# TensorE's signals raised by a drain of its sequencer, in a graph network of four layers

## The chip, the cores and the metric

One NeuronCore of one Trainium2 chip runs the whole program. The metric is the device time of one execution in microseconds (us); lower is better. The core has five engines that run side by side, each with its own queue of instructions: PE (TensorE, matrix products), DVE (VectorE), ACT (ScalarE), POOL (GpSimd) and SP (SyncE, which here only issues DMAs). They wait for each other by semaphores.

## The reference

`x` holds 6,250 nodes of 128 values; there are 106,250 edges with `src`, `dst` (sorted by `dst`) and one of 40 types. Each of four layers computes `x = LayerNorm(x + layer(x))`:

- layer 0, relations: `S = segment_sum(x[src], dst * 40 + type)`, then `sum over r of S[:, r] @ W[r]` plus `cnt @ rFeatures`, times `deg ** -0.5`, then `relu(h + h @ loop)`;
- layer 1, attention with 4 heads of 64: a softmax over the edges of each target, with `segment_max` as its maximum, weighted `segment_sum`, relu, a product by `fc_w`;
- layer 2, attention with 4 heads of 32, with one global maximum, a skip, elu;
- layer 3, six rounds of routing on 8 capsules of 16 values: `p = softmax(sum(z * u[dst]))` per edge with `z = xk[src]`, `u = normalize(segment_sum(z * p, dst) + xk)`.

## The kernel before

The edges are laid into 880 chunks of 128 slots (`NCH`), taken four at a time: a *quad* (`CQ = 4`, `NQ = 220`). A gather or scatter by index is an indirect DMA that POOL issues, one per chunk. A sum over targets is a product on PE of a 0/1 matrix (*hots*, made from `dst`) by the rows of the chunk. Most buffers exist four times (`RING`), indexed by `s = q % 4`. `sweep()` (L53) writes out the order on each engine: for each quad it calls the stage functions, each at an offset of so many quads. A function waits on its semaphores, issues, and lets its last instruction raise one. The program's order on each engine is this written order.

The five stages that the diff touches (letters are this document's):

- **A, the products of layer 0** (L451 to L510). For each of 50 node tiles, ACT copies the tile to `xs` (L480), PE transposes it (L491, raises `s_xtp`), ACT copies it to `xt` (L484), and PE makes ten products of 128 x 512 (L497, each raises `s_y`) into four PSUM banks in turn; product n waits for the addition of n - 4 (`s_yc`). DVE adds the relation features (L509) into `y_out`, and SP stores two additions at a time (L463) to `y_tab`. On POOL, beside this and independent of it, 831 scatters (L472) write the edge records.
- **B, the sums of layer 0** (L749 to L827). POOL gathers the edges' rows of `y_tab` (L562), DVE makes hots (L599), PE's `total` multiplies four chunks (L827, raises `s_sum` once a quad), DVE adds each chunk's sum to its target tile (L813).
- **C, the maximum of layer 1** (`source_maximum`, L1012 to L1124). POOL gathers (L1035), ACT packs (L1088), PE's `turn` transposes (L1108, `s_turn`), ACT copies a line (L1096), PE's `spread` makes for each chunk four products (L1118) and one (L1121, `s_spread` per chunk), DVE reduces each chunk (L1067). PE's order is turn of q + 1, spread of q.
- **D, layer 2's sweep** (`attend_once`, L1413 to L1564). PE's order for quad q: `expand` of q + 1 (L1532, `s_exp`), `turn` of q + 1 (L1542, `s_turn`), `lanes` of q (L1548, `s_row`), `spread_top` (L1552, `s_bc`), `total` (L1561, `s_sum`). Between them DVE needs expand for `sent` (L1440), the scores and their maximum over lanes (L1454), PE turns that to a row, DVE takes the running maximum (L1458, L1461), PE spreads it, ACT makes the exponential, DVE the messages (L1468), then comes the total. POOL gathers ahead (L562), as buffers come free.
- **E, round one of layer 3** (`first_round`, L1796 to L1970). PE's order: `total` of q - 1 (L1963, `s_sum`), `turn` of q + 1 (L1953, `s_turn`), `expand` of q + 2 (L1942, `s_exp`). POOL gathers `z` (L1827), DVE makes products, sums and messages (L1845, L1865) and adds (L1881), ACT widens, exponentiates and scales hots (L1904, L1912, L1922).

In all five POOL issues indirect DMAs. The stages without them (the sweep over kept rows in layer 1, rounds two to six of layer 3 with L2227 and L2239, the projections) are not touched. A `drain` of an engine is an instruction of its sequencer that stands in the program's order behind the others; before the change the touched blocks have one on each engine at their end only.

Of the kernel before, what the change touches and what calls it, by code (L numbers as in the profile page):

```python
# [14 lines left out]
P = 128  # L15
# [68 lines left out]
def gnn_resnorm_kernel(nc, x_in, src_in, dst_in, type_in, rfeat, relw, loopw,  # L84
# [3 lines left out]
    with ctx:  # L88
# [59 lines left out]
        with Phase() as ph:  # L148
# [302 lines left out]
            with nc.Block() as block:  # L451
                @block.sync
                def _(sp):
                    sp.dma_start(w0[:], relw.rearrange("r d f -> d r f")).then_inc(s_w, 16)
                    sp.dma_start(rf_b[:], rfeat.rearrange("r d -> (r d)").unsqueeze(0).broadcast_to([P, R * D]))\
                      .then_inc(s_w, 16)
                    sp.wait_ge(s_w, 32)


                    for d in range(NTP * GRP // 2):  # L460
                        t, c = d // (GRP // 2), d % (GRP // 2)
                        sp.wait_ge(s_yc, 2 * d + 2)
                        sp.dma_start(y_view[t:t + 1, :, c * 1024:(c + 1) * 1024].rearrange("t p w -> (t p) w"),  # L463
                                     y_out[:, d % 2].rearrange("p a w -> p (a w)")).then_inc(s_yo[d % 2], 16)
                    for s in range(2):
                        sp.wait_ge(s_yo[s], 16 * (NTP * GRP // 4))

                @block.gpsimd
                def _(pool):

                    for j in range(EJ):
                        nc.gpsimd.indirect_dma_start(  # L472
                            out=rec_tab, out_offset=bass.IndirectOffsetOnAxis(ap=row_i[:, j:j + 1], axis=0),
                            in_=pay[:, j, :], in_offset=None).then_inc(s_sc, 16)
                    pool.wait_ge(s_sc, 16 * EJ)

                @block.scalar
                def _(act):
                    for t in range(NTP):
                        nc.scalar.activation(xs[:], x_sb[:, t, :], ACT.Copy).then_inc(s_xs, 1)  # L480
                        act.wait_ge(s_xtp, t + 1)
                        if t > 0:
                            act.wait_ge(s_y, t * GRP)
                        nc.scalar.activation(xt[:], ps[:, 7, 0:P], ACT.Copy).then_inc(s_xt, 1)  # L484

                @block.tensor
                def _(pe):
                    pe.wait_ge(s_w, 32)
                    for t in range(NTP):
                        pe.wait_ge(s_xs, t + 1)  # L490
                        nc.tensor.transpose(ps[:, 7, 0:P], xs[:], ident[:]).then_inc(s_xtp, 1)  # L491
                        pe.wait_ge(s_xt, t + 1)
                        for g in range(GRP):
                            n = t * GRP + g
                            if n > 3:
                                pe.wait_ge(s_yc, n - 3)
                            nc.tensor.matmul(ps[:, n % 4, :], xt[:], w0[:, 4 * g:4 * g + 4, :],  # L497
                                             start=True, stop=True).then_inc(s_y, 1)

                @block.vector  # L500
                def _(dve):
                    v = nc.vector
                    dve.wait_ge(s_w, 32)
                    for n in range(NTP * GRP):
                        g, d = n % GRP, n // 2
                        dve.wait_ge(s_y, n + 1)
                        if n % 2 == 0 and d >= 2:
                            dve.wait_ge(s_yo[d % 2], 16 * (d // 2))
                        v.tensor_tensor(y_out[:, d % 2, n % 2, :], ps[:, n % 4, :],  # L509
                                        rf_b[:, g * 512:(g + 1) * 512], ALU.add).then_inc(s_yc, 1)  # L510
# [220 lines left out]
        with Phase() as ph:  # L731
# [17 lines left out]
            with nc.Block() as block:  # L749
# [69 lines left out]
                @block.tensor  # L819
                def _(pe):  # L820
                    def total(q, s):
                        pe.wait_ge(s_hot, q + 1)
                        pe.wait_ge(s_gath[s], gathered(q, s))
                        if not isinstance(q, int) or q >= 2:
                            pe.wait_ge(s_acc, (q - 1) * CQ)
                        for c in range(CQ):
                            last = nc.tensor.matmul(ps[:, (s % 2) * CQ + c, 0:W], hots[:, s, c, :], ring[:, s, c, :],  # L827
                                                    start=True, stop=True)
                        last.then_inc(s_sum, 1)
                    sweep(pe, [(0, total)], straight=True)  # L830


# [146 lines left out]
        def source_maximum(name, f, t_tab, keep_tab, most):  # L979
# [5 lines left out]
            with Phase() as ph:  # L985
# [26 lines left out]
                with nc.Block() as block:  # L1012
# [86 lines left out]
                    @block.tensor  # L1099
                    def _(pe):  # L1100
                        pe.wait_ge(s_ini, 2)

                        def turn(q, s):
                            pe.wait_ge(s_pack, q + 1)
                            if not isinstance(q, int) or q >= 2:
                                pe.wait_ge(s_line, q - 1)
                            pe.sem_inc(s_tick, 1)
                            nc.tensor.transpose(turned(s), parts[:, s, :], ident_b[:])\  # L1108
                              .then_inc(s_turn, 1)

                        def spread(q, s):
                            pe.wait_ge(s_line, q + 1)
                            pe.wait_ge(s_oth, q + 1)
                            for c in range(CQ):
                                if not isinstance(q, int) or q >= 1:
                                    pe.wait_ge(s_red, (q - 1) * CQ + (c + 1))
                                for h in range(HEADS):
                                    nc.tensor.matmul(ps[:, c, h * P:(h + 1) * P], pick[:, c * HEADS + h, :],  # L1118
                                                     lines[:, s, :], start=h == 0, stop=False)

                                nc.tensor.matmul(ps[:, c, :], others[:, s, c, :],  # L1121
                                                 far[:].rearrange("p h e -> p (h e)"), start=False, stop=True)\
                                  .then_inc(s_spread, 1)
                        sweep(pe, [(1, turn), (0, spread)], straight=True)  # L1124

        def target_rows(name, ph, a_src, a_dst, most, exp_n, own):
# [228 lines left out]
        def attend_once(name, f, t_tab, a_dst, last_neg, top_neg):  # L1355
# [6 lines left out]
            with Phase() as ph:  # L1362
# [50 lines left out]
                with nc.Block() as block:  # L1413
# [109 lines left out]
                    def _(pe):  # L1523
# [3 lines left out]
                        def expand(q, s):  # L1527
# [3 lines left out]
                            for c in range(CQ):  # L1531
# [1 line left out]
                                    ps[:, 6 + s % 2, c * HW:(c + 1) * HW], ohts[:, s, c * P:(c + 1) * P],  # L1533
                                    exp_n[:, bass.ds(tiles[s, c], 1), :, :].rearrange("p t k w -> p (t k w)"),
                                    start=True, stop=True)
                            last.then_inc(s_exp, 1)

                        def turn(q, s):
                            if not isinstance(q, int) or q >= 2:
                                pe.wait_ge(s_hot, q - 1)  # L1540
                            for c in range(CQ):
                                last = nc.tensor.transpose(turned(s)[:, c * P:(c + 1) * P],  # L1542
                                                           ohts[:, s, c * P:(c + 1) * P], ident_b[:])
                            last.then_inc(s_turn, 1)

                        def lanes(q, s):
                            pe.wait_ge(s_lt, q + 1)
                            nc.tensor.transpose(lane_row(s), lane_top[:, s, :], ident[:]).then_inc(s_row, 1)  # L1548

                        def spread_top(q, s):  # L1550
                            pe.wait_ge(s_rt, q + 1)
                            nc.tensor.matmul(spread(s), one_row[:], run_top[0:1, s:s + 1], start=True, stop=True)\  # L1552
                              .then_inc(s_bc, 1)

                        def total(q, s):
                            pe.wait_ge(s_m, q + 1)
# [3 lines left out]
                            for c in range(CQ):  # L1560
                                last = nc.tensor.matmul(sums(s, c), hots[:, s, c, :], msg[:, s, c, :],  # L1561
                                                        start=True, stop=True)
                            last.then_inc(s_sum, 1)
                        sweep(pe, [(1, expand), (1, turn), (0, lanes), (0, spread_top), (0, total)], tiles, straight=True)  # L1564


# [144 lines left out]
        with Phase() as l3:  # L1711
# [47 lines left out]
            def first_round(name):  # L1759


                with Phase() as ph:
# [33 lines left out]
                    with nc.Block() as block:  # L1796
# [136 lines left out]
                        def _(pe):  # L1933
                            def body(r):
                                tiles = Tiles(PE_ENGINE, 2)

                                def expand(q, s):
# [3 lines left out]
                                    for c in range(CQ):  # L1941
# [1 line left out]
                                            ps[:, s, c * D:(c + 1) * D], wide[:, s, c * P:(c + 1) * P],  # L1943
                                            unit[:, bass.ds(tiles[s, c], 1), :].rearrange("p t w -> p (t w)"),
                                            start=True, stop=True)
                                    last.then_inc(s_exp, 1)

                                def turn(q, s):
                                    pe.wait_ge(s_ohl[s], r * per + loaded(q, s))
# [2 lines left out]
                                    for c in range(CQ):  # L1952
                                        last = nc.tensor.transpose(turned(s)[:, c * P:(c + 1) * P],  # L1953
                                                                   ohts[:, s, c * P:(c + 1) * P], ident_b[:])
                                    last.then_inc(s_turn, 1)

                                def total(q, s):
                                    pe.wait_ge(s_msg, r * NQ + (q + 1))
# [3 lines left out]
                                    for c in range(CQ):  # L1962
                                        last = nc.tensor.matmul(ps[:, 4 + s % 2, c * D:(c + 1) * D], hots[:, s, c, :],  # L1963
                                                                msg[:, s, c * D:(c + 1) * D], start=True, stop=True)
                                    last.then_inc(s_sum, 1)
                                sweep(pe, [(-1, total), (1, turn), (2, expand)], tiles, straight=True)
                            body(0)

# [340 lines left out]
```

## Time and profile before

| | |
|---|---|
| median of 3 runs | 11,336.08 us (11,329.6 to 11,339.88) |
| the profiled execution | 11,339.56 us, of which the span 11,337.8 us |
| busy share of the span | PE 60%, DVE 57%, POOL 57%, PE's weight loads 45%, ACT 22% |
| mean granted clock of PE | 0.703 of full speed |
| L562 POOL gathers of B | 881.7 us busy (1,002 ns each), 726.4 us idle before them |
| L472 POOL scatters of A | 842.3 us busy (1,014 ns each) |
| L497 PE products of A | 607.2 us busy, 821.8 us idle before them |
| L509 DVE additions of A | 330.9 us busy, 1,124.8 us idle before them, 794.4 of it "remote" |

"Idle before" is the time an engine sat idle just ahead of those instructions, with what ended most of it; idle time of an engine that is not the bottleneck costs nothing. "issue" means that the engine waited for nothing that the profile shows, "remote" that a semaphore was waited for whose sender was not found. Two matmul records belong to one fp32 product.

### The profile page before, as it was taken

Reading aid. Unit: us, or ns where it says so; the run is one execution under the profiler, and the core shown is the slowest. Engines: PE = TensorE matmul, PEld = TensorE weight load, DVE = VectorE, ACT = ScalarE, POOL = GpSimd, SP = SyncE. Lnnn points to the kernel's source line nnn. Section 1 sums busy time; section 2 is a strip of 40 time slices with the busy share of each in tenths; the row PEclk is TensorE's granted clock in tenths of the full one; section 3 lists DMA queues with packets and bytes.
Section 4 is the critical chain, followed back from the end, with each engine's and each line's share of the span. In section 5 each row is a group of like instructions: output and inputs, shape, how many; then the busy total and the mean of one; then the engine's idle time right before and its main releaser. Section 6 shows DMA issues by size and latency. Waiting matters only on the chain. (4 is left out here: it accounts for less than half of the span.)

```text
span 11337.8 us, 161595 instructions
## 1 busy us (share of the span) xinstructions
PE 6767.9 (60%) x41381; PEld 5071.3 (45%) x41382; DVE 6482.6 (57%) x18631; ACT 2515.4 (22%) x6766; POOL 6430.9 (57%) x5741
## 2 busy tenths in 40 slices
PE   4422256333337777688745555345444698898986
PEld 3200022333323333344434444244444698898986
DVE  7411135555555555677754444534444688888888
ACT  0000000000010000022211111133333455555554
POOL 0477732777726666444235555255555587787876
PEclk9755577555565555599865555577776899999998
DMA  0111135555546666655322222233333566666664
GB/s 22 58 47 46 46 145 184 117 115 117 113 80 172 176 175 176 167 181 182 115 53 62 61 61 62 40 97 97 95 97 96 145 210 186 186 210 187 209 186 149
DMA packets 1109223, 1395.56 MB, mean 123 GB/s; under 512 B 277691, under 2 KB 974351, under 8 KB 1108111
## 3 DMA queue, kind: packets, MB, share of 16 engines
q1 hardware_dynamic: 955182, 1090.46, 31.1%
q0 software_dynamic: 153312, 296.65, 12.9%
q8 instruction: 304, 4.98, 0.2%
q14 instruction: 425, 3.47, 0.1%
HBM read 1002.58 MB, written 383.96 MB: 122 GB/s over the span
## 5 line engine op out<-in xcount | busy, mean ns | idle before, releaser
L562 POOL DMA_INDIRECT ring_e<-t_tab,src_row x880 | 832.4, 946 | 825.6 <-DVE msg_e L1468 424.1
L1827 POOL DMA_INDIRECT z_r<-x_tab,src_row x880 | 839.4, 954 | 805.6 <-DVE msg_r L1865 405.1
L562 POOL DMA_INDIRECT ring<-y_tab,y_row x880 | 881.7, 1002 | 726.4 <-DVE ring L783 356.5
L472 POOL DMA_INDIRECT rec_tab<-pay,row_i x831 | 842.3, 1014 | 694.5 <-POOLq L202 402.1
L2227 PE MATMUL ps<-u,wide_r 128*128 x9280 | 1141.4, 277 | 126.2 <-issue 88.7
L2239 PE MATMUL ps<-msg_r,hots_r 128*128 128x128 f32 x9280 | 1150.8, 277 | 105.4 <-POOL msg_r L2060 104.7
L2060 POOL TENSOR_TENSOR msg_r<-zo_r,share_r 128x1024 f32<-128x1024 f32 x580 | 1122.8, 1936 | 87.5 <-DVE share_r L2119 13.7
L2227 PEld LDWEIGHTS ps<-u,wide_r 128*128 128x128 f32 x9280 | 1093.0, 194 | 128.2 <-issue 128.2
L2239 PEld LDWEIGHTS ps<-msg_r,hots_r 128*128 128x128 f32 x9280 | 1083.2, 192 | 138.4 <-POOL msg_r L2060 137.7
L1035 POOL DMA_INDIRECT ring_m<-t_tab,src_row x880 | 850.5, 966 | 516.7 <-ACT slot_parts_m L1088 262.9
L497 PE MATMUL ps<-w,xt 128*128 128x512 f32 x1000 | 607.2, 747 | 821.8 <-issue 503.7
L2068 POOL TENSOR_TENSOR prod_r<-prod_r 128x512 f32<-128x512 f32 x580 | 735.1, 1267 | 437.4 <-DVE prod_r L2091 425.1
L509 DVE TENSOR_TENSOR y_out<-ps,rf_b 128x512 f32<-128x512 f32 x500 | 330.9, 689 | 1124.8 <-remote 794.4
L827 PE MATMUL ps<-ring,hots 128*128 128x129 f32 x1760 | 458.6, 442 | 835.4 <-issue 561.1
L1067 DVE TENSOR_REDUCE high_m<-ps 128x4 f32<-128x512 f32 x880 | 588.9, 685 | 623.4 <-PE ps L1121 348.3
L827 PEld LDWEIGHTS ps<-ring,hots 128*128 128x128 f32 x1760 | 394.1, 329 | 900.1 <-issue 679.0
L497 PEld LDWEIGHTS ps<-w,xt 128*128 128x128 f32 x1000 | 207.4, 228 | 1202.8 <-issue 672.4
L1118 PE MATMUL ps<-lines_m,pick_m 48*128 48x128 bf16 x3520 | 530.5, 304 | 350.2 <-DVE high_m L1067 273.5
L2091 DVE TENSOR_TENSOR prod_r<-ps,zo_r 128x1024 f32<-128x1024 f32 x580 | 707.9, 1221 | 33.3 <-PE ps L2227 30.8
L2130 DVE TENSOR_TENSOR u_sum<-ps,u_sum 128x128 f32 x2320 | 667.4, 288 | 89.5 <-PE ps L2239 40.2
L1561 PE MATMUL ps<-msg_e,hots_e 128*128 128x132 f32 x1760 | 468.2, 447 | 333.9 <-DVE msg_e L1468 333.9
L1963 PE MATMUL ps<-msg_r,hots_r 128*128 128x128 f32 x1760 | 341.4, 355 | 509.9 <-DVE msg_r L1865 395.2
(320 smaller groups left out, 13430.4 us busy)
## 6 DMA issues: line engine op xcount, KB each, us to landing
zo_r<-zo_tab SPq DMA_DIRECT2D x2320, 192.0 KB
y_tab<-y_out SPq DMA_DIRECT2D x250, 512.0 KB
k_tab<-ring_m SPq DMA_DIRECT2D x220, 520.0 KB
ring_e<-k_tab SPq DMA_DIRECT2D x220, 520.0 KB
ohts_e<-oht_tab SPq DMA_DIRECT2D x440, 128.0 KB
zo_tab<-z_r SPq DMA_DIRECT2D x220, 256.0 KB
dl_b<-dl_tab SPq DMA_DIRECT2D x220, 128.0 KB
oht_tab<-ohts SPq DMA_DIRECT2D x220, 128.0 KB
```

The costliest lines, as they stand in the source:

```text
L472: nc.gpsimd.indirect_dma_start(out=rec_tab, out_offset=bass.IndirectOffsetOnAxis(ap=row_i[:, j:j + 1], axis=0), in_=pay[:, j, :], in_offse ...
L497: nc.tensor.matmul(ps[:, n % 4, :], xt[:], w0[:, 4 * g:4 * g + 4, :], start=True, stop=True).then_inc(s_y, 1)
L562: nc.gpsimd.indirect_dma_start(out=ring[:, s, c, 0:width], out_offset=None, in_=table, in_offset=bass.IndirectOffsetOnAxis(ap=rows[:, q * ...
L827: last = nc.tensor.matmul(ps[:, (s % 2) * CQ + c, 0:W], hots[:, s, c, :], ring[:, s, c, :], start=True, stop=True)
L1035: nc.gpsimd.indirect_dma_start(out=ring[:, s, c, :], out_offset=None, in_=t_tab, in_offset=bass.IndirectOffsetOnAxis(ap=src_row[:, q * CQ ...
L1827: nc.gpsimd.indirect_dma_start(out=z[:, s, c * D:(c + 1) * D], out_offset=None, in_=x3_tab, in_offset=bass.IndirectOffsetOnAxis(ap=src_row ...
L2060: nc.gpsimd.tensor_tensor(msg[:, g % WR].rearrange("p c (k d) -> p c k d", d=CD), z_of(g).rearrange("p c (k d) -> p c k d", d=CD), share[: ...
L2068: nc.gpsimd.tensor_tensor(prod[:, :, 0:CD // 2], prod[:, :, 0:CD // 2], prod[:, :, CD // 2:CD], ALU.add).then_inc(s_half, 1)
L2091: v.tensor_tensor(prod[:].rearrange("p (c k) d -> p c (k d)", k=CAPS), up, z_of(g), ALU.mult).then_inc(s_prod, 1)
L2130: v.tensor_tensor(t, ps[:, 4 + g % 2, a * D:(a + 1) * D], t, ALU.add)\
L2227: last = nc.tensor.matmul(ps[:, 2 * (g % 2) + c // 4, c % 4 * D:(c % 4 + 1) * D], wide[:, g % WR, c, :], u[:, bass.ds(tiles[g % NO % 4 * O ...
L2239: last = nc.tensor.matmul(ps[:, 4 + g % 2, c // 2 * D:(c // 2 + 1) * D], hots[:, g % WR, c, :], msg[:, g % WR, c, :], start=c % 2 == 0, st ...
```

## The change

In the five stages every `then_inc` on a matmul or transpose is removed, and a `nc.tensor.drain()` behind it raises the same semaphore by the same amount. Order, waits, operands and all other engines are as they were. The drains number 50 + 500 in A, 220 in B, 220 + 880 in C, 5 x 220 in D and 3 x 220 in E.

```diff
@@ stage A: the products of layer 0 @@
-                        nc.tensor.transpose(ps[:, 7, 0:P], xs[:], ident[:]).then_inc(s_xtp, 1)
+                        nc.tensor.transpose(ps[:, 7, 0:P], xs[:], ident[:])
+                        nc.tensor.drain().then_inc(s_xtp, 1)
...
                             nc.tensor.matmul(ps[:, n % 4, :], xt[:], w0[:, 4 * g:4 * g + 4, :],
-                                             start=True, stop=True).then_inc(s_y, 1)
+                                             start=True, stop=True)
+                            nc.tensor.drain().then_inc(s_y, 1)
@@ stage B: total @@
                             last = nc.tensor.matmul(ps[:, (s % 2) * CQ + c, 0:W], hots[:, s, c, :], ring[:, s, c, :],
                                                     start=True, stop=True)
-                        last.then_inc(s_sum, 1)
+                        nc.tensor.drain().then_inc(s_sum, 1)
@@ stage C: turn, and spread (once a chunk) @@
-                            nc.tensor.transpose(turned(s), parts[:, s, :], ident_b[:])\
-                              .then_inc(s_turn, 1)
+                            nc.tensor.transpose(turned(s), parts[:, s, :], ident_b[:])
+                            nc.tensor.drain().then_inc(s_turn, 1)
...
                                 nc.tensor.matmul(ps[:, c, :], others[:, s, c, :],
-                                                 far[:].rearrange("p h e -> p (h e)"), start=False, stop=True)\
-                                  .then_inc(s_spread, 1)
+                                                 far[:].rearrange("p h e -> p (h e)"), start=False, stop=True)
+                                nc.tensor.drain().then_inc(s_spread, 1)
@@ stage D: expand, turn, lanes, spread_top, total @@
-                            last.then_inc(s_exp, 1)
+                            nc.tensor.drain().then_inc(s_exp, 1)
...
-                            last.then_inc(s_turn, 1)
+                            nc.tensor.drain().then_inc(s_turn, 1)
...
-                            nc.tensor.transpose(lane_row(s), lane_top[:, s, :], ident[:]).then_inc(s_row, 1)
+                            nc.tensor.transpose(lane_row(s), lane_top[:, s, :], ident[:])
+                            nc.tensor.drain().then_inc(s_row, 1)
...
-                            nc.tensor.matmul(spread(s), one_row[:], run_top[0:1, s:s + 1], start=True, stop=True)\
-                              .then_inc(s_bc, 1)
+                            nc.tensor.matmul(spread(s), one_row[:], run_top[0:1, s:s + 1], start=True, stop=True)
+                            nc.tensor.drain().then_inc(s_bc, 1)
...
-                            last.then_inc(s_sum, 1)
+                            nc.tensor.drain().then_inc(s_sum, 1)
@@ stage E: expand, turn, total: the same three lines (s_exp, s_turn, s_sum) @@
```

## Rows read from the trace of the kernel before

**Rows 1.** The table of windows of the stages A to E: start:end, length, each engine's busy time, PEclk the granted clock

```profile
422.00:1858.00 1436.00, 614.54 (x1049) 215.95 (x1049) 328.80 (x497) 23.28 (x98) 829.58 (x819) 0.65 0.24 92
1897.00:3170.00 1273.00, 458.65 (x1760) 394.10 (x1760) 670.75 (x1756) 0.00 (x0) 881.54 (x880) 0.50 0.53 113
3347.00:4730.00 1383.00, 1015.11 (x4620) 418.14 (x4620) 759.22 (x1985) 89.10 (x440) 850.51 (x880) 0.50 0.65 172
5786.00:7255.00 1469.00, 796.38 (x4180) 638.76 (x4180) 671.05 (x3294) 253.25 (x881) 820.45 (x868) 0.50 0.28 60
7374.00:8896.00 1522.00, 735.12 (x4400) 663.70 (x4400) 631.45 (x1760) 543.33 (x2863) 839.43 (x880) 0.70 0.37 96
```

**Rows 2.** The list of waits of stage A: engine, line, releaser, total us, times, longest

```profile
DVE y_out L509 <- remote: 794.4, 164, 5.6
```

**Rows 3.** Timeline of stage A: start, us, engine, line, operation, idle before and releaser

```profile
966.46 0.28 ACT L484 ACTIVATE xt<-ps 128x128 f32<-128x128 f32 x1 [58.33 <-remote]
...
998.67 0.69 DVE L509 TENSOR_TENSOR y_out<-ps,rf_b 128x512 f32<-128x512 f32 x1 [4.92 <-remote]
...
999.42 2.08 PE L497 MATMUL ps<-w,xt 128*128 128x512 f32 x2 [3.53 <-DVE y_out L509]
...
1004.26 0.69 DVE L509 TENSOR_TENSOR y_out<-ps,rf_b 128x512 f32<-128x512 f32 x1 [4.90 <-remote]
...
1021.06 0.69 DVE L509 TENSOR_TENSOR y_out<-ps,rf_b 128x512 f32<-128x512 f32 x1 [4.90 <-remote]
...
1025.26 0.28 ACT L484 ACTIVATE xt<-ps 128x128 f32<-128x128 f32 x1 [58.33 <-remote]
```

**Rows 4.** Timeline of the end of stage A

```profile
1539.35 0.97 POOL L472 DMA_INDIRECT rec_tab<-pay,row_i  x1 [0.30 <-issue]
...
1621.72 2.62 DVE L509 TENSOR_TENSOR y_out<-ps,rf_b 128x512 f32<-128x512 f32 x4 [1.36 <-DMA y_tab<-y_out]
...
1622.66 7.49 PE L497 MATMUL ps<-w,xt 128*128 128x512 f32 x16 [0.37 <-ACT xt L484]
1623.19 0.19 PEld L497 LDWEIGHTS ps<-w,xt 128*128 128x128 f32 x1 [0.24 <-DVE y_out L509]
```

**Rows 5.** The list of waits of stage B

```profile
POOL ring L562 <- remote: 109.3, 38, 3.6
```

**Rows 6.** Drains at the end of a block: ns min/median/max, first to last start

```profile
L451 POOLq DRAIN  x1: 8020/8020/8020, 1542.8 to 1542.8; - x1
...
L1012 PEldq DRAIN  x1: 3340/3340/3340, 4726.5 to 4726.5; - x1
```

**Rows 7.** Stage C: a line of its waits, and the timeline of PE at its end

```profile
POOL ring_m L1035 <- ACT slot_parts_m L1088: 262.9, 100, 16.3
...
4727.59 0.61 PE L1118 MATMUL ps<-lines_m,pick_m 48*128 48x128 bf16 x4
...
4728.66 0.61 PE L1118 MATMUL ps<-lines_m,pick_m 48*128 48x128 bf16 x4
4729.20 0.61 PE L1121 MATMUL ps<-far_m,others_m 128*128 128x512 bf16 x1
```

**Rows 8.** Stage D: timeline of one quad, and expand's register operations by line

```profile
6501.81 2.13 PE L1561 MATMUL ps<-msg_e,hots_e 128*128 128x132 f32 x8 [1.51 <-DVE msg_e L1468]
6503.51 0.42 PEld L1532 LDWEIGHTS ps<-exp_n_e,ohts_e 128*128 128x128 bf16 x4
6503.73 0.30 PE L1532 MATMUL ps<-exp_n_e,ohts_e 128*128 x4
...
6504.07 0.21 DVE L1440 TENSOR_REDUCE sent_e<-ps 128x16 f32<-128x48 f32 x1 [2.31 <-PE ps L1532]
...
L1532 PEldq FUSED_REGOPS  x880: 46/46/52, 5786.5 to 7240.1; - x176
```

**Rows 9.** Stage E: a line of its waits, and PE's timeline in the middle

```profile
POOL z_r L1827 <- DVE msg_r L1865: 405.1, 88, 6.8
...
7916.19 0.37 PE L1942 MATMUL ps<-unit,wide_r 128*128 x1 [1.83 <-issue]
```

More of the change, by code:

```diff
@@ L1945, in expand @@
                                             start=True, stop=True)
-                                    last.then_inc(s_exp, 1)
+                                    nc.tensor.drain().then_inc(s_exp, 1)
                                 def turn(q, s):
@@ L1954, in turn @@
                                                                    ohts[:, s, c * P:(c + 1) * P], ident_b[:])
-                                    last.then_inc(s_turn, 1)
+                                    nc.tensor.drain().then_inc(s_turn, 1)
                                 def total(q, s):
@@ L1964, in total @@
                                                                 msg[:, s, c * D:(c + 1) * D], start=True, stop=True)
-                                    last.then_inc(s_sum, 1)
+                                    nc.tensor.drain().then_inc(s_sum, 1)
                                 sweep(pe, [(-1, total), (1, turn), (2, expand)], tiles, straight=True)
```

## The prediction

> **What bounds the kernel now.** I first cut the span into its stages by a table of windows, then read in each stage the list of waits, and where a wait needed explaining the timeline around one quad (four chunks of 128 edge slots). The diff touches five stages, A to E, with 7,083 of the 11,337.8 us [rows 1]; the rest is untouched and is carried over as it is.
>
> *A, the products of layer 0.* DVE's largest wait is 794 us in 164 pieces of up to 5.6 us, put down to "remote", a signal whose sender the profile cannot find [rows 2]. The timeline shows it: the product of 999.42 ends at 1001.50, but banks are read in turn, and the addition that follows that product, four banks behind, starts at 1021.06; additions come 5.60 us apart [rows 3]. The work is done, the news of it is late. ACT's copies of one tile and the next stand 58.80 us apart [rows 3], for ten products (two matmuls and two weight loads each) and one transpose (one and one): 42 PE instructions, 1.40 us each, and a product's four give the 5.60. So it is one PE instruction released every 1.40 us, whether it carries a signal (one in four) or not. It lasts a little beyond POOL's last indirect scatter at 1539.35; then additions come four to a run, 3.98 us apart, held by the stores [rows 4]. Between 448 and 1549 us some 1,101/5.60 = 197 products pass at the slow pace.
>
> *B and C.* POOL's gathers set B: 880 of them take 1.00 us with 0.30 us of issue between them, some 5.2 us a quad of the stage's 5.79, and 109 us of its idle time is "remote" [rows 1, 4, 5]. In C it is the ACT line behind a late turn: POOL waits 263 us for slot_parts [rows 7], at 6.29 us a quad.
>
> *D* has no late signal in its chain: sent_e of the next quad starts 0.04 us after expand's end [rows 8]. It is a chain PE, DVE, PE, DVE, PE, DVE, PE, at 6.68 us a quad. *E* stands between: POOL waits 405 us for msg_r, and PE itself starts single matmuls some 2 us apart, five in a row around 7,916 us, with "issue" before them and no semaphore at all [rows 9].
>
> **The decision.** A drain is a sequencer instruction. Two readings. Either only the matmul's own update message is late, then the drain, which doesn't ride on a matmul, goes out at once; or the completions of PE's instructions come in late, then a drain that waits for them is as late, and adds that nothing may be issued meanwhile. For the first: DVE, ACT and POOL show no late updates; only what hangs on a PE instruction is late. For the second: the plain matmuls of [rows 9], of which three in four carry no update, are stalled too, and A's unit of 1.40 us fits all instructions (42 a tile), not the 11 that carry an update [rows 3]. And POOL's drain at the end of A lasts 8.02 us, with its last scatter ended at 1540.32 [rows 4] and 2.5 us more until it began [rows 6]: an engine's drain can wait for something that no row shows. PE's own drain at the end of C, when no transfer is left, ends at 4729.84, 0.03 us behind the last matmul's modelled 4729.81 [rows 6, 7]: at rest it costs next to nothing. I lean to the second.
>
> The Trainium skill, PSUM — Partial Sum Buffer, Engine vs sequencer instructions, says to attach the increment to the matmul, since an engine-attached update fires on completion, and that a drain waits until the engine is idle. By that rule alone every drain would only cost; the trace contradicts its first half in A (20 us late), and the second half is what I bet on.
>
> **The change, part by part.** It adds 3,630 drains: A 50 + 500, B 220, C 220 + 880, D 5 x 220, E 3 x 220, and takes nothing from any engine but an update. No DMA is moved; SP and POOL get no new instruction.
>
> A, late stretch. If the drain counts as one more instruction of 1.40 us, 5.60 becomes 7.00: in 1,101 us 157 products are done instead of 197, and 40 are left for later at 1.0 us, +40. If it doesn't, its wait for the four before it is the 5.60 us there is: 0. Taken +20.
> A, fast stretch. 16 matmuls run in 7.49 us, 0.94 a product, with the loads beside them; the pace is 3.98/4 = 1.00, held by the stores [rows 4]. With a drain the next load can't be pulled ahead: 0.94 + 0.19 for a load at this clock + 0.05 for the drain = 1.18. The 285 additions from 1566 to 1858 us have one product each: at most +51; I take +40, since buffers of finished banks absorb some. Lower end 0. A: **+60**.
>
> B. POOL binds at 5.2 us a quad; PE's matmuls are busy for 459 of 1,273 us [rows 1]. A quad has 16 PE instructions (1,760 matmuls and as many loads over 220 quads); a 17th, if the crawl were the bound, would add 5.79/16 = 0.36 us a quad, 80 us. Ends 0 and +80, taken **+40**: only part of the stage crawls.
>
> C. A chunk's pace on PE is 1.07 us [rows 7]; a chunk on its own takes 1.15 (4728.66 to 4729.81), plus 0.05 for the drain and up to 0.04 for its wait: 0.13 to 0.17 more, 880 times, and some 0.25 for each turn: 115 to 205 us if PE binds. PE's own quad is 4 x 1.07 plus a turn, about 4.6 of 6.29, so at rest the slack hides it (0); in late stretches it doesn't. Taken in the middle: **+110**.
>
> D. Here the drain lies on the chain of every quad. Expand's first load now starts at 6503.51, before the total's eight matmuls end at 6503.94 [rows 8]. With a drain behind the total it starts at 6503.99: +0.48. Its four register operations, 46 ns each [rows 8], are no longer hidden: +0.18. Its own drain +0.05, and the same for lanes, spread_top and total, which each release DVE on the chain: +0.15. Sum 0.86 us x 220 = **+185**. The low end is 4 x 0.05 x 220 = 44, if the loads can still be hidden; the high end adds a cold refill of the pipeline after each, 0.95 x 220 = 209. This term does not depend on which reading holds. If the drain is itself late, what it costs is in the range.
>
> E. The same exposed load and drain as in D would be 0.8 x 220 = 175; but expand and turn run one or two quads ahead, so the total alone is on the chain, and POOL (839 of 1,522 us busy [rows 1]) has slack of its own. Ends 0 and +175; halfway, **+90**.
>
> Sum 60 + 40 + 110 + 185 + 90 = +485: 11,337.8 + 485 + 1.8 us outside the span = 11,825 for the profiled execution, which is 3.5 over the median of 11,336.1: **11,820** on its scale. This case's own range is 11,450 (half of D and a little of C) to 12,150 (upper ends: 91 + 80 + 205 + 209 + 175 = +760, and late drains on D's chain).
>
> **Rivals.**
> *The drain escapes entirely (faster).* Mechanism: the sequencer's update doesn't pass the clogged path, in A first of all. A then ends when scatter and products end: the last scatter at 1540.3, POOL's drain until 1550.8, products at the lower clock 2.08 [rows 3] and some 0.3 (an estimate) for load and drain, 2.4 us, 500 of them from some 405 = about 1,600 at worst: -270. B gives back its remote wait: -110. C goes to PE's pace with drains, 4.6 + 0.7, and half a us of POOL's and ACT's hand-over, 5.8: -110. D stays +185. E goes from 6.92 to POOL's 5.2 and the same half us, 5.8: -250. Sum -555: **10,780**. Point of decision: additions of A no longer 5.60 us apart. For it: the first reading. Against it: the stalled matmuls of [rows 9].
> *Signals leave on time, PE's own queue still crawls (slower, small).* The readers wait no longer, but PE issues its next entry at the old pace: A 0 in the late stretch and +40 in the fast one, B -30, C 0, D +185, E -50: +145, **11,485**. For it: [rows 9] shows a stall of issue, not of a signal.
> *It doesn't do what it says.* If gains of the first and D's cost cancel, or the drain is hidden everywhere but its gain too, the time stays within 23 us. Nothing but coincidence speaks for it: **11,340**.
> The skill's page Perfetto Trace Analysis lists DRAIN among the sequencer's own instructions, whose update goes out when they execute; this speaks for the first rival, but doesn't say whether completions it waits for can be late.
>
> **How the numbers follow.** Measurement tells 0.2%, 23 us, from no change. Chances: forecast 0.45, small slower rival 0.16, faster rival 0.33, same 0.06. So faster 0.33, same 0.06, slower 0.61. The range must hold both signs: from 10,650 (the faster rival, 135 better at D's low end of 44) to 12,150, which leaves out a tenth on either side.
>
> **What would show it.** In A: "remote" gone from xt and y_out and the stage over by 1,600 us means the faster rival; additions 5.6 to 7.0 us apart and the end at 1,860 or later, the forecast. PE's drains in A of 5 us and more say that they wait for late completions; 0.1 us says they don't. In D: sent_e about 0.7 us later after the total, the quad at 7.4 to 7.5 us, both for the forecast and the faster rival; a D below 6.9 would sink the one term that all cases share. In C: chunks 1.2 us apart. In E: whether matmuls 2 us apart with "issue" are still there; if they are gone, it was the pending updates that held them and my argument for late completions was wrong.

## The result and the profile after

The changed kernel takes 11,674.4 us (11,651.6 to 11,694.2, 4 runs) against 11,338.0 us (4 runs of the kernel before): a ratio of 1.0295, interval 1.028 to 1.031, 336 us slower. Slower was forecast, by 485 us.

The windows of the same five stages after [rows 1], with the same columns:

```profile
422.00:1949.00 1527.00, 767.35 (x1049) 196.67 (x1049) 345.14 (x500) 23.36 (x99) 817.24 (x819) 0.63 0.23 87
1985.00:3254.00 1269.00, 456.15 (x1760) 394.09 (x1760) 668.14 (x1755) 0.00 (x0) 883.25 (x880) 0.50 0.52 114
3431.00:4860.00 1429.00, 1062.15 (x4620) 418.23 (x4620) 804.10 (x1984) 88.77 (x440) 833.95 (x880) 0.50 0.62 167
5898.00:7646.00 1748.00, 944.01 (x4180) 694.47 (x4180) 684.27 (x3302) 252.95 (x881) 829.97 (x880) 0.50 0.22 51
7765.00:9230.00 1465.00, 964.00 (x4400) 801.14 (x4400) 638.85 (x1757) 543.12 (x2863) 835.54 (x880) 0.56 0.38 99
```

Measured from the first scatter or gather of a stage to the end of PE's drain that closes its block, A went from 1,452 to 1,543 us (+91), B from 1,272 to 1,268 (-3), C from 1,383 to 1,429 (+46), D from 1,484 to 1,748 (+263), E from 1,520 to 1,464 (-56). They sum to +341; between the stages it is 5 us less.

**A.** The list of waits of A after answers to [rows 2], and the timeline around 1,000 us to [rows 3]:

```profile
DVE y_out L511 <- PEq L500: 1148.6, 478, 19.9
ACT xt L484 <- issue: 1019.3, 19, 58.3
```

```profile
996.87 0.69 DVE L511 TENSOR_TENSOR y_out<-ps,rf_b 128x512 f32<-128x512 f32 x1 [4.91 <-PEq L500]
996.89 0.50 PEld L498 LDWEIGHTS ps<-w,xt 128*128 128x128 f32 x2 [5.10 <-issue]
996.89 2.07 PE L498 MATMUL ps<-w,xt 128*128 128x512 f32 x2 [3.53 <-issue]
...
1002.47 0.69 DVE L511 TENSOR_TENSOR y_out<-ps,rf_b 128x512 f32<-128x512 f32 x1 [4.91 <-PEq L500]
```

The word "remote" has gone from DVE's waits and PE's sequencer is named (L500 is the drain) instead, and nothing else has changed: the additions are still 5.60 us apart. The product of 996.89 ends at 998.96; its drain lets go at 1002.47 (that is when the addition starts), 3.5 us later. What changed is the order: before, four products were in flight and each was known 20 us late; now one is in flight and is known 3.5 us late. The rate, four PE instructions per 5.60 us, is that of the completions. A renamed wait is not a wait gone.

The drains' own rows, one line of the source each (ns min/median/max, first to last start):

```profile
L500 PEldq DRAIN  x500: 942/1102/5512, 422.2 to 1947.8; - x167
L831 PEldq DRAIN  x220: 1930/3065/15765, 1992.5 to 3251.5; - x110
L1125 PEldq DRAIN  x880: 941/1125/11763, 3446.5 to 4858.5; - x176
L1538 PEldq DRAIN  x220: 187/188/3295, 5915.4 to 7632.7; - x110
L1566 PEldq DRAIN  x220: 2130/2133/2133, 5925.8 to 7643.8; - x110
L1949 PEldq DRAIN  x220: 605/1667/6442, 7777.1 to 9220.3; - x110
L1968 PEldq DRAIN  x220: 1130/2045/7585, 7792.2 to 9227.4; - x110
```

A drain's duration holds the work it stands behind, so the maxima tell: 5.5 us in A, 15.8 in B, 11.8 in C, 6.4 and 7.6 in E (expand, total). Behind D's total the longest equals the median, 2.13 us, which are the eight matmuls. D is the one stage in which nothing is late, but for one of its 1,100 drains, of 3.3 us behind expand at its very start.

D issues as many indirect DMAs as the others, 880, but never more than four in a row, with a wait between, after a first run of 16. In B the gathers come in runs of about 24. Counted there drain by drain (a gap of under 1 us between two gathers doesn't end a run): of the 94 drains that end while up to seven gathers of a run have been issued, none ends more than 0.3 us behind its last matmul; of the 71 with twelve or more, 64 do, by 4.6 us in the median. In E, behind expand, it is 1 of 124 with up to three gathers issued and 76 of 84 with four or more. So on this chip lateness builds up along a run of indirect DMAs, and short runs escape it. This is counted, not tested by an experiment.

A's end is the fast stretch, here once lateness has gone, answering to [rows 4]:

```profile
1591.08 0.69 DVE L511 TENSOR_TENSOR y_out<-ps,rf_b 128x512 f32<-128x512 f32 x1 [0.51 <-PEq L500]
1592.28 0.69 DVE L511 TENSOR_TENSOR y_out<-ps,rf_b 128x512 f32<-128x512 f32 x1 [0.51 <-PEq L500]
1594.20 0.69 DVE L511 TENSOR_TENSOR y_out<-ps,rf_b 128x512 f32<-128x512 f32 x1 [1.23 <-PEq L500]
```

A product now takes 1.20 us and, at a new tile, 1.92 lie between two additions; the stores no longer bind.

**D.** The timeline after of one quad and the next expand, answering to [rows 8], and the register loads of tile numbers by their line:

```profile
6703.44 2.13 PE L1564 MATMUL ps<-msg_e,hots_e 128*128 128x132 f32 x8 [1.53 <-DVE msg_e L1470]
6707.06 0.23 PEld L1534 LDWEIGHTS ps<-exp_n_e,ohts_e 128*128 128x128 bf16 x2 [1.80 <-issue]
6707.06 0.72 PE L1534 MATMUL ps<-exp_n_e,ohts_e 128*128 x4 [1.50 <-issue]
...
6707.84 0.21 DVE L1442 TENSOR_REDUCE sent_e<-ps 128x16 f32<-128x48 f32 x1 [4.46 <-PEq L1538]
```

```profile
L591 PEldq TENSOR_LOAD <-chunk_tile x64: 331/1107/1115, 5914.5 to 7631.7; - x64
```

Expand's load used to start 0.43 us before the total's end; it now starts 1.49 us behind 6705.57. That is more than the drain. In this quad the sequencer loads 16 tile numbers into registers, 1.11 us from 6705.69 on, once for every four quads: 52 times, and 12 times four numbers in 0.33 us for the single quads at both ends. It always did, but while the matmuls still ran.

### The profile page after: what moved, and what is told of

Read it like the earlier page. It is cut to its first block and busy times, and to the rows that moved or that the text cites. A ratio compares the mean times of both kernels' runs of the same rounds, so it can differ in the third digit from the quotient of the medians.

```text
span 11673.6 us, 165225 instructions
## 1 busy us (share of the span) xinstructions
PE 7341.9 (63%) x41381; PEld 5244.2 (45%) x41382; DVE 6546.8 (56%) x18631; ACT 2513.4 (22%) x6766; POOL 6395.0 (55%) x5741
## 5 line engine op out<-in xcount | busy, mean ns | idle before, releaser
L2242 PE MATMUL ps<-msg_r,hots_r 128*128 128x128 f32 x9280 | 1152.2, 277 | 104.6 <-POOL msg_r L2063 104.0
L498 PE MATMUL ps<-w,xt 128*128 128x512 f32 x1000 | 748.7, 839 | 690.2 <-issue 652.3
L1204 POOL TENSOR_TENSOR msg_e<-ring_e,msg_e 128x768 f32<-128x768 f32 x220 | 323.7, 1471 | 556.5 <-ACT msg_e L1310 556.5
```

Source lines behind the costliest of these rows:

```text
L2242: last = nc.tensor.matmul(ps[:, 4 + g % 2, c // 2 * D:(c // 2 + 1) * D], hots[:, g % WR, c, :], msg[:, g % WR, c, :], start=c % 2 == 0, st ...
```

## The experiments

The same kernel ran in two kinds of surroundings. In one (here: the late chips, with the prediction's numbers) the kernel before takes 11,338 to 11,354 us. In the other (the prompt chips) it takes 10,239 to 10,245. The experiments landed on three chips, one late and two prompt, each visited once; that it is the chip and not the moment is the likely reading, not a shown one. D, and all that lies between and behind the stages, is equal on both to a few us; A, B, C and E are not. A stretch of time that a run gives for a stage it doesn't touch is used below as that of the kernel before. From first scatter or gather to the end of PE's drain that closes the block, us; for A on a prompt chip to the end of POOL's, since the scatters end last there:

| stage | late: before | late: changed | late: bare drains | prompt: before | prompt: bare drains |
|---|---|---|---|---|---|
| A | 1,452 | 1,543 | 1,543 | 1,075 | 1,073 |
| B | 1,272 | 1,268 | 1,272 | 1,161 | 1,163 |
| C | 1,383 | 1,429 | 1,427 | 1,156 | 1,241 |
| D | 1,484 | 1,748 | 1,728 | 1,480 | 1,725 |
| E | 1,520 | 1,464 | 1,483 | 1,142 to 1,153 | 1,161 |

The late bare drains ran beside a second run of the changed kernel, on a late chip on which the kernel before takes 11,354 us (whether it is the chip of the first two columns is not known). Stages that the runs there don't touch give the kernel before 1,376 and 1,379 us for C, 1,484 for D, 1,528 and 1,531 for E; the changed kernel took 1,434, 1,748 and 1,468 there. So E's gain came twice, there with some 60 us.

On a prompt chip the late signals are absent. Here are A's waits there, in a kernel whose A is the one before, and the time of the scatters there; the row behind them is of bare drains behind the products:

```profile
ACT xt L484 <- PE ps L491: 484.8, 49, 13.3
...
DVE y_out L509 <- DMA y_tab<-y_out: 182.6, 216, 3.7
```

```profile
L472 POOL DMA_INDIRECT rec_tab<-pay,row_i x831: 953/959/1147, 405.1 to 1474.6; - x167
```

```profile
L500 PEldq DRAIN  x500: 1007/1147/2123, 421.8 to 1070.3; - x167
```

The scatters take 1.29 us each, start to start, instead of 1.36; products are done by 940 us, and the longest drain is 2.1 us, the product at the lower clock.

**Who raises the signal.** Bare drains, signals left where they were:

```
                             nc.tensor.matmul(ps[:, n % 4, :], xt[:], w0[:, 4 * g:4 * g + 4, :],
                                              start=True, stop=True).then_inc(s_y, 1)
+                            nc.tensor.drain()
```
(and so at all 13 places)

> All signals stay on the matmuls and transposes as before; behind each a drain without a signal is added, at the places of the changed kernel's drains. Theory T1 (what costs and gains is that PE may not run ahead; by whom the signal is raised makes no difference, since PE's completions themselves come in late): the same as the changed kernel, 11,674 within 25 us, stage by stage: A +91, B -3, C +46, D +263, E -57 against the kernel before. Rival T2 (the drain's signal travels another way than the matmul's, and E's gain of 57 us comes from that): E loses its gain or turns slower, and the stages come out by tens of us otherwise than in the changed kernel. If the attached signals are late on their own account, readers of A would wait longer than 5.60 us a product.

Measured: 10,583.1 us against 10,239.2, ratio 1.0337 (1.032 to 1.0354), on a prompt chip; the absolute figures expected don't apply. The changed kernel had to be run beside it.

> The changed kernel itself once more, since the runs above came from a chip on which the kernel before takes 10,239 us instead of 11,338, with the stages A, B, C and E shorter by 366, 111, 226 and 378 us and no late signals in A. Theory T1: where signals are not late, the drains still cost D its 245 us, C 80, E 20, and nothing in A (its 500 products end well before the scatters): ratio 1.033 to 1.035 on such a chip, equal to the kernel with bare drains in the same call within 0.1%. T2 (who raises the signal matters): differs from it by more than 0.2%.

> Bare drains behind attached signals, now on the same chip as the changed kernel. T1: the same time as the changed kernel within 0.1 to 0.2%, in every stage within 10 us. T2: a stage with other numbers.

Measured side by side, on a late chip: changed 11,684.6 us, ratio 1.0287 (1.027 to 1.0305); bare drains 11,681.8 us, ratio 1.0294 (1.0276 to 1.0311). As a whole they are the same. By stages the expectation of 10 us was missed twice, in opposite directions: D is 20 us shorter with the signals on the matmuls (1,728 against 1,748), that is 0.09 us a quad for its five signals, and E is 15 longer (1,483 against 1,468 on that chip). In A both give 5.60 us a product; with bare drains the timeline reads

```profile
1005.98 0.69 DVE L511 TENSOR_TENSOR y_out<-ps,rf_b 128x512 f32<-128x512 f32 x1 [4.91 <-remote]
1011.58 0.69 DVE L511 TENSOR_TENSOR y_out<-ps,rf_b 128x512 f32<-128x512 f32 x1 [4.91 <-remote]
```

So what the change did is the draining; the way of the signal is worth 0.09 us a quad in D.

**Where D's cost sits.** The changed kernel, with one drain of five taken back:

```
-                            nc.tensor.drain().then_inc(s_sum, 1)
+                            last.then_inc(s_sum, 1)
```

> The changed kernel, but in stage D the total's signal is attached to its last matmul again and no drain stands behind it; the four other drains of D stay. Theory T1 (D's +263 us is the drain behind the total: it exposes expand's weight load and register operations, 0.66 us a quad, and every fourth quad a register load of tile numbers, 1.1 us): D is at most 0.2 us a quad longer than before the change, 20 to 60 us instead of 263; the whole about 11,440 to 11,480. Rival T2 (each drain on the chain costs the same, about a fifth of 1.2 us a quad): D stays at +210, the whole at 11,620.

Measured on a prompt chip: 10,335.0 us, 248 us below the bare drains on the same chip; D 1,490 us against 1,480 before and 1,725 with all five. (The 11,440 to 11,480 expected was for a late chip; 20 to 60 us for D's four drains was too much.) The timeline shows expand's load again ahead of the total's end (6007.74):

```profile
6005.61 2.13 PE L1564 MATMUL ps<-msg_e,hots_e 128*128 128x132 f32 x8 [1.53 <-DVE msg_e L1470]
6007.31 0.42 PEld L1534 LDWEIGHTS ps<-exp_n_e,ohts_e 128*128 128x128 bf16 x4
6007.53 0.30 PE L1534 MATMUL ps<-exp_n_e,ohts_e 128*128 x4
6007.89 0.21 DVE L1442 TENSOR_REDUCE sent_e<-ps 128x16 f32<-128x48 f32 x1 [2.33 <-PEq L1538]
```

Four drains a quad cost 10 us in all, the fifth 235. A drain's price is what it keeps from being fetched and loaded ahead. The bare drains differ from the changed kernel in who signals, but the table puts that at 20 us, not at 235.

**Whether E's gain stands alone.** B and E with their drains, the rest as before; then E alone; then E's parts (the edits are those of the diff in these places):

> Drains in stages B and E only; A, C and D as before the change. Theory T1 (stages don't act on each other, and E's gain is the drains' own): B -3, E -57, the rest 0: 11,278, ratio 0.995. Rival (E was shorter only because it began in another state of the DMA queue or the clock after a longer D): E keeps its 1,520 us and the whole is 11,330 to 11,345.

> Drains in stage E alone (round one of layer 3), 660 of them. On a chip with late signals T1 (E's gain of 52 to 57 us is its own drains' doing and independent of the longer stages before it): E 1,465 to 1,485 us instead of 1,520 to 1,531, the whole 0.4 to 0.5% faster, ratio 0.995 to 0.996. Rival: E's gain came from what A to D left behind: ratio 1.000. On a chip without late signals: about 20 us slower, ratio 1.002.

> Drains in E behind the total alone (220). T6 (the gain comes from a PE that does not queue turn and expand behind a total whose completion is late, so that the total's own signal goes out sooner): all of E's gain, 40 to 60 us. Rival T8 (it comes from the drain behind expand, which keeps the next total's loads from being queued behind 16 uncompleted instructions): nothing, or some 20 us slower.

> Drains in E behind turn and expand alone (440), the total's signal attached as before. T8: all of E's gain, 40 to 60 us. T6: nothing, or slower by up to 20 us.

All four ran on prompt chips, where there is no lateness to gain from: 10,250.7 us, ratio 1.001 (1.0 to 1.002); 10,256.9 us, 1.0013 (1.0003 to 1.0022); 10,251.2 us, 1.0005 (0.9995 to 1.0014); 10,243.7 us, 1.0 (0.999 to 1.0009). E took 1,162, 1,162, 1,154 and 1,151 us against 1,142 to 1,153. So all three drains cost E 9 to 20 us where nothing is late, about what was expected there, and one or two of them nothing that stands out of the 11 us between the two times of E before. Which of them brings E's gain on a late chip was not measured; T6 against T8 stays open, and so does whether drains in E alone beat the kernel before on a late chip.

**What makes completions late.** At most four scatters in the queue (`OUT = 4`):

```
+                        if j >= OUT:
+                            pool.wait_ge(s_out[j % OUT], 16 * (j // OUT))
...
-                            in_=pay[:, j, :], in_offset=None).then_inc(s_sc, 16)
+                            in_=pay[:, j, :], in_offset=None).then_inc(s_out[j % OUT], 16)
```

> The kernel before, with one edit in stage A: POOL issues a scatter only when the fourth before it has landed (four semaphores in turn), so that at most four are in the queue; before, about 17 were. No drain is added. Theory T3 (PE's completions come in late only while a long backlog of indirect DMAs stands in the software queue, and then one PE instruction per scatter, 42 of each in 58.8 us): additions come at 1.0 to 2.2 us instead of 5.60, products are done after at most 1,100 us, and A ends when scatters end, by 1,560 to 1,700 us instead of 1,858: the whole 11,040 to 11,180. Rival T4 (any indirect DMA in flight delays PE's completions, backlog or not): additions stay near one product per four scatters, A ends no earlier, or later by as much as POOL is slowed: 11,336 to 11,700.

Measured on a prompt chip: 10,228.3 us, ratio 0.9991 (0.9981 to 1.0), A 1,060 against 1,075. POOL waited for a landing only 10 times, 7 us in all, so even without the limit there are seldom more than four in the queue; the "about 17" of the expectation stands in no row. Where nothing is late, it shows nothing of lateness. So I added work to make the queue slow, a second scatter of 128 rows of 2 KB behind each of the first 300, and ran it with and without the limit; they landed on a late chip.

```
+                            nc.gpsimd.indirect_dma_start(
+                                out=wide_tab, out_offset=bass.IndirectOffsetOnAxis(ap=wide_row[:, j:j + 1], axis=0),
+                                in_=wide_in[:], in_offset=None).then_inc(s_sc, 16)
```

> The kernel before; in stage A behind each of the first 300 scatters comes a second one that writes 128 rows of 2 KB to a table nobody reads (extra work, about 840 us of it). T3 (PE's completions come in late when the software queue drains slower than POOL fills it): with the wide rows the queue is slower than POOL, so late completions appear also on a chip that has none otherwise: additions of L509 evenly spaced, at four queue entries a product, waits put down to remote, as long as the wide scatters last; after their end additions return to about 1.0 us. Rival T4 (the lateness is a property of the other chip that has nothing to do with the backlog): additions stay at 1.0 us apart or are held by the stores alone.

> As the kernel with wide scatters, but POOL issues one only when the fourth before it has landed, so that the queue never holds more than four. T3 with the backlog as the cause: the lateness is gone or much smaller (additions 1 to 2 us apart), the scatters take as long as without the limit, since the queue stays busy. T5 (what counts is that the queue is busy, not how much stands in it): additions as late as without the limit.

Measured, one run each: 11,694.3 and 11,707.1 us against 11,354.4. DVE's timeline without the limit, then with it:

```profile
999.41 0.69 DVE L526 TENSOR_TENSOR y_out<-ps,rf_b 128x512 f32<-128x512 f32 x1 [4.91 <-remote]
1005.00 0.69 DVE L526 TENSOR_TENSOR y_out<-ps,rf_b 128x512 f32<-128x512 f32 x1 [4.90 <-remote]
```

```profile
1002.41 0.69 DVE L530 TENSOR_TENSOR y_out<-ps,rf_b 128x512 f32<-128x512 f32 x1 [4.91 <-remote]
1008.00 0.69 DVE L530 TENSOR_TENSOR y_out<-ps,rf_b 128x512 f32<-128x512 f32 x1 [4.90 <-remote]
```

Both again 5.60 us, and so on until the last scatter, at 1,964 and 1,968 us. Rows 128 times as wide change nothing. The limit of four changes nothing either, but it made POOL wait for a landing only 4 times in 1,131, 7 us in all: with it never more than four scatters had not yet landed, and without it seldom. Additions were late all the same, so lateness needs no long backlog of scatters that have not landed, which is what T3 supposed, and T3 in this form falls. That the queue is what counts at all (T5) is not shown by it. What the runs do show is that lateness lasts as long as indirect DMAs are issued one behind the other, whatever they carry. The next expectation's "5.80 us apart" is 5.60 in these rows.

> The kernel before with one edit in A: POOL issues a scatter only when the one before it has landed; never more than one is in flight, and there is a stretch with none between two. With at most four in flight nothing had changed: additions 5.80 us apart, a scatter every 1.40 us. T9 (PE's instructions complete freely as soon as no indirect DMA is in flight): products pass at 1 to 2.2 us in spite of scatters that now come 2 us or more apart; the 500 products are done by 1,100 to 1,500 us, A ends with the scatters. T10 (one PE instruction completes for each indirect DMA, whatever lies between): additions come at four times the scatters' new distance, 8 us or more, and A is longer by hundreds of us.

Measured on a third chip, again a prompt one: 11,252.7 us against 10,244.9, the scatters 2.49 us apart on average. Products took 1.0 us as before, done by 940 us, so it doesn't tell T9 from T10; it only puts a price on waiting for each landing, about 1.2 us a scatter.

## Why the prediction was right, and where its sizes were off

**The decision: right.** It was made for the second reading, that PE's completions are late and a drain waits for them. The drain of A that lasts 5.5 us, the unchanged 5.60 us, and the bare drains with the same time show it. What is late is the completion, so an update that fires on completion is late with it: against the prediction's own sentence, A does not contradict that rule. The faster rival is out: "remote" went from the list, but not one us of A's waiting. My argument from counting (42 instructions a tile, one per 1.40 us) held against the other, that only updates are late. One sign of mine came out against me: the single matmuls of E with "issue" before them, 1.2 to 2.6 us apart, were 158 before and are 0 after, which I had called proof that pending updates held them. It is no such proof: with bare drains every update is on its matmul as before, and they are 0 too; in B, where the kernel before has 105 of them, 107 and 102 are left.

**A, +60 forecast, +91 measured.** The late stretch: near the lower of the two ends; a drain is no entry and 5.60 stays 5.60. The fast stretch was undersized. The additions still to come at 1,567 us are 287 before and 298 after. Before they take 1.02 us each, after 1.28 (nine at 1.20 and one at 1.92 a tile): 287 x 0.26 = 75, and 11 more at 1.28 = 14, which the late stretch left behind. I had 0.18 a product as the exposed load and took off from it; the 1.92 at each tile was not in the sum.

**B, +40 forecast, -3.** The lower end: the gathers still come in runs of about 24 and bind as before, and a drain is no extra entry. **C, +110 forecast, +46:** between its ends. A chunk on PE now takes 1.22 us, as forecast. On the prompt chip, where POOL is quicker and PE binds, the same drains cost 84 us; on the late chip POOL and late completions cover part of them.

**D, +185 forecast, +263: the term that was mis-sized.** The step "expand's first load starts at 6503.99; its four register operations are no longer hidden" was right as far as it went: most quads take 7.49 us instead of 6.61, 0.88 where I had 0.86 (which times 220 is 189, not the 185 of the sum). It left out the one register load of 1.11 us that stands before expand in every fourth quad. On average the 167 quads without it take 7.57 us, the 52 with it 8.71, and before all take 6.64: 167 x 0.93 + 52 x 2.07 = 155 + 108 = 263. The register load is 52 x 1.14 = 59 of that. The register load was in the trace of before, under the line that loads tile numbers, and the prediction has no row of it. These are the quads, by DVE's sent_e:

```profile
6691.57 0.21 DVE L1442 TENSOR_REDUCE sent_e<-ps 128x16 f32<-128x48 f32 x1 [3.17 <-PEq L1538]
6699.06 0.21 DVE L1442 TENSOR_REDUCE sent_e<-ps 128x16 f32<-128x48 f32 x1 [3.16 <-PEq L1538]
...
6715.38 0.21 DVE L1442 TENSOR_REDUCE sent_e<-ps 128x16 f32<-128x48 f32 x1 [3.22 <-PEq L1538]
```

7.49 us lie between the first two; the one of 6707.84, shown above, comes 8.78 behind the second.

**E, +90 forecast, -56: the sign was wrong.** The small slower rival had -50 for it, on the reasoning that signals would leave on time. They don't: E's drain behind expand lasts up to 6.4 us. The gain is the draining's (with bare drains E is 1,483, also below 1,520), and shows only where completions are late (on prompt chips the drains cost 9 to 20 us). It came in spite of a lower granted clock, 0.56 against 0.70 [rows 1], at which the same 4,400 matmuls are busy 964 us instead of 735. What else changed in E is how POOL issues. Before, and then after:

```profile
7914.09 0.27 PE L1942 MATMUL ps<-unit,wide_r 128*128 x1 [1.07 <-issue]
7918.27 0.37 PE L1942 MATMUL ps<-unit,wide_r 128*128 x1 [1.72 <-issue]
7923.52 0.94 POOL L1827 DMA_INDIRECT z_r<-x_tab,src_row  x1 [6.11 <-DVE msg_r L1865]
```

```profile
8390.20 0.94 POOL L1830 DMA_INDIRECT z_r<-x_tab,src_row  x1 [2.64 <-DVE msg_r L1868]
8396.86 2.07 PE L1945 MATMUL ps<-unit,wide_r 128*128 x8 [0.56 <-issue]
8403.78 0.94 POOL L1830 DMA_INDIRECT z_r<-x_tab,src_row  x1 [3.41 <-DVE msg_r L1868]
```

Before, POOL gathered twelve times in a row (7902.71 to 7916.47) and then waited; there are 63 such runs in the stage, and the stalled matmuls here stand at the end of one; after, its runs are of eight (68) or four (50). Shorter runs mean less lateness, by the counts above, and in B the runs stay at 24 and the time stays too. This fits E's gain, but no run separates it from others: a PE that drains also has at most one group of 8 to 16 instructions waiting to complete, where before it ran two groups ahead of the total.

The sum of the terms came out 149 us too high because B, C and E together were 253 too high and A and D 109 too low; the last 5 lie between the stages. That the total lies no farther off is in part luck: it is the difference of misses that partly cancel.

## What to carry to other kernels

A wait that the profile can't name may be a completion that is late; moving the signal to another instruction only renames it. Before a drain is put on a chain, list what the sequencer does ahead of time behind it, register loads and weight loads included, at their full duration: here one drain of five cost 235 us and the other four 10. And a stage's stalls may belong to the chip one measures on: the four stages with long runs of indirect DMAs differed by up to 26% between chips, while all the drains together cost about 3% on both. A gain of a few per cent in such a stage is to be repeated on more than one chip.

## What the runs showed of the hardware

While POOL issues indirect DMAs back to back, PE's instructions on some chips complete one per 1.40 us, 42 of them per 42 scatters in 58.8 us, whether a scatter's rows hold 16 bytes or, in every second one, 2 KB, and with no more than four not yet landed. With four in a row and a pause (D) they complete on time. On other chips the same kernel shows none of it, even in runs of more than 800 gathers in B and C, and is 1,100 us faster. A drain of PE ends 0.02 to 0.05 us behind the last matmul when completions are prompt, and with them when they are late: in A's late stretch a product takes 5.60 us with it and without. Why completions are late, and why on some chips only, these runs don't tell.
